# A fused patch-matching and FFN kernel: one-operation squares, relu on ScalarE, and a new call order

## The reference

```python
x = x + conv_ref(ln_c(x), ...)       # match, argmax, gather, mix, 4 small layers
t = to_tokens(x)
t = t + ffn(ln_t(t))                 # ln_t: mean and variance over the 96 channels
# ffn: h = relu(q_acc(q_acc(q_mul(x) @ q_mul(W1).T) + q_mul(b1)))
#      y = q_acc(q_acc(q_mul(h) @ q_mul(W2).T) + q_mul(b2))
```

## Time and profile before

| | |
|---|---|
| median of 3 runs | 2088.41 us (2086.51 to 2092.78) |
| profiled execution | 2092.94 us, of which the span is 2090.8 us |
| mean granted TensorE clock | 0.981 of full speed |
| VectorE busy | 2003.2 us, 96% of the span |
| TensorE busy | 1957.4 us, 94% |
| ScalarE busy | 1829.2 us, 87% |
| GpSimd busy | 1549.9 us, 74% |
| DMA | mean 92 GB/s |
| chain that ended last | 89% on VectorE |

### The profile page before, as it was taken

One profiled execution on the slowest core, in us unless ns is written; L12 is line 12 of the kernel. 1 busy time (PEld: TensorE's weight loads), 2 busy tenths in 40 slices (PEclk: granted clock), 3 DMA queues, 4 the chain that ended last, 5 costly groups with the idle time before them and its releaser, 6 DMA issues.

```text
span 2090.8 us, 46997 instructions
## 1 busy us (share of the span) xinstructions
PE 1957.4 (94%) x13105; PEld 1434.5 (69%) x13105; DVE 2003.2 (96%) x6781; ACT 1829.2 (87%) x5381; POOL 1549.9 (74%) x1042
## 2 busy tenths in 40 slices
PE   5899999999999999999999999999999999999975
PEld 4677777777777777767777777777777777777653
DVE  7999999999999999999999999999999999999953
ACT  1179999999999999999999999999999999999997
POOL 2577877878778777787887777878778778787753
PEclk9999999999999999999999999999999999999985
DMA  3322232332322323323233232232332322323111
GB/s 89 97 78 88 94 106 87 98 102 87 108 91 95 105 87 102 97 91 110 86 97 103 87 107 92 95 105 87 102 97 93 108 86 98 103 87 111 46 40 51
DMA packets 65475, 193.27 MB, mean 92 GB/s; under 512 B 13689, under 2 KB 15939, under 8 KB 65219
## 3 DMA queue, kind: packets, MB, share of 16 engines
q1 hardware_dynamic: 52866, 170.80, 25.2%
q0 software_dynamic: 10240, 18.89, 3.0%
q10 hardware_dynamic: 2112, 0.60, 0.1%
HBM read 133.23 MB, written 57.02 MB: 91 GB/s over the span
## 4 chain that ended last, share of the span: by engine, by line
DVE 89%; issue 6%; PE 3%; ACT 1%; POOL 0%; DMA 0%; POOLq 0%; ACTq 0%; DVEq 0%
DVE best_y L1026 28%; DVE h L1043 13%; DVE stats L1035 9%; DVE t_pm L1051 6%; DVE simraw L1077 6%; DVE top_v L1065 4%; DVE w_index L1072 4%; DVE zb L992 3%; DVE xn L984 1%; DVE mix_in L971 1%; DVE m_dif L929 1%; DVE r_u L1010 1%; DVE ra L1018 1%; DVE one_j L903 1%; DVE r_t L1015 1%
## 5 line engine op out<-in xcount | busy, mean ns | idle before, releaser
L1026 DVE TENSOR_REDUCE best_y<-y_ps 128x2 f32<-128x1024 f32 (+1 forms) x640 | 692.7, 1103 | 4.0 <-PE y_ps L651 3.9
L466 ACT CAST y<-bank 128x384 f16<-128x384 f32 x1152 | 550.5, 478 | 140.8 <-PE bank L674 129.8
L649 PE MATMUL y_ps<-proto_hi,xh 96*128 96x512 f32 x1152 | 553.8, 481 | 22.2 <-DVE best_y L1026 10.4
L359 POOL TENSOR_TENSOR tq<-t_dev,ra 128x864 fp8e5<-128x864 f32 x128 | 209.5, 1637 | 401.3 <-DVE ra L1018 401.3
L650 PE MATMUL y_ps<-proto_lo,xh 96*128 96x512 f32 x1152 | 458.4, 398 | 0.0
L651 PE MATMUL y_ps<-proto_hi,xl 96*128 96x512 f32 x1152 | 457.3, 397 | 0.0
L475 ACT ACTIVATE h<-h 128x1152 fp8e5<-128x1152 f16 x384 | 448.3, 1168 | 0.0
L674 PE MATMUL bank<-tqt,f_w 96*128 96x384 f16 x1152 | 390.4, 339 | 26.5 <-ACT y L466 24.6
L403 POOL TENSOR_TENSOR xl<-xc,xh 96x1152 fp32r<-96x1152 f32 x128 | 339.7, 2654 | 26.4 <-ACT xh L536 15.2
L1043 DVE TENSOR_SCALAR h<-y,f_b 128x1152 f16<-128x1152 f16 x384 | 306.1, 797 | 21.0 <-ACT y L466 20.9
L505 ACT ACTIVATE sq_junk<-t_dev 128x96 f32<-128x96 f32 x1152 | 318.8, 289 | 0.9 <-POOL t_dev L371 0.9
(11 more groups left out here) (131 smaller groups left out, 3997.3 us busy)
## 6 DMA issues: line engine op xcount, KB each, us to landing
xc<-x_cm SPq DMA_DIRECT2D x128, 432.0 KB, 4.0
xp<-x_pm SPq DMA_DIRECT2D x128, 432.0 KB, 4.8
out<-o_pm SPq DMA_DIRECT2D x128, 432.0 KB, 2.5
xsel<-x_pm,x_index POOLq DMA_INDIRECT x128, 2.5
wsel<-proto_rows,w_index POOLq DMA_INDIRECT x128, 4.9
proto_rows<-proto SPq DMA_DIRECT2D x1, 384.0 KB, 2.6
proto<-w_mask SPq DMA_DIRECT2D x1, 192.0 KB, 3.4
f_f<-w_1t ACTq DMA_DIRECT2D x1, 144.0 KB
```

Of the source, the lines that this page charges most:

```text
L466: act.copy(y16[:, q, r, 0:TOK], bank[0][:, 0:TOK]).then_inc(s_y16, 1)
L649: pe.matmul(y, hi, proto_hi[:], start=True, stop=False)
L1026: dve.tensor_reduce(best_y[t % 2][:, j0:j1], y_ps[n % 2][:, 0:j1 - j0, :], AX_X, ALU.max).then_inc(s_yd, 1)
```

## The change

Three edits. The nine squares of a tile on ScalarE, each with a sum read from an accumulator, become one square of all 864 values into t_sq, and VectorE sums them with one reduction (`t_squares`). For q = 0 and 1, bias and relu move from VectorE (`ffn_bias`) to ScalarE (`hidden16`); q = 2 stays on VectorE. And the calls in `slot(s)` of four engines stand in another order; SyncE's order is the same.

```diff
+            def hidden16(s, stage, q):
+                if run.live(s, stage):
+                    t = s - stage
+                    run.wait(s_y16, NC * t + 3 * (q + 1))
+                    run.wait(s_h8, NH * (t - 1) + q + 1)
+                    run.apart()
+                    act.activation(h16[:, q, :, 0:P].rearrange("p (r j) l -> p r j l", r=3),
+                                   y16[:, q, :, 0:TOK].rearrange("p r (j l) -> p r j l", l=P), ACT.Relu,
+                                   bias=f1_b[:, q:q + 1]).then_inc(s_h16[q], 1)
...
-            def squares(s, js):
+            def squares(s):
...
-                        ins = act.activation(sq_junk[:, j * C:(j + 1) * C], t_dev[t % 2][:, j * C:(j + 1) * C],
-                                             ACT.Square, accum_out=va[(s + 1) % 2][:, J + j:J + j + 1])
...
+                    run.wait(s_dev, t + 1)
+                    run.wait(s_sqd, t)
+                    run.apart()
+                    act.activation(t_sq[:], t_dev[t % 2][:], ACT.Square).then_inc(s_sq, 1)
...
+            def t_squares(s):
+                if run.live(s, NORM):
+                    run.wait(s_sq, s - NORM + 1)
+                    ins = dve.tensor_reduce(va[s % 2][:, J:2 * J], t_sq[:].rearrange("p (j c) -> p j c", c=C), AX_X, ALU.add)
+                    ins.then_inc(s_sqd, 1)
...
             def slot(s):
                 lock(s)
                 t_norm(s)
                 product(s)
+                low_h(s)
                 t_center(s)
+                low_x(s)
                 gather_x(s)
+                gather_w(s)
                 output(s)
-                low_x(s)
-                low_h(s)
-                gather_w(s)
```

More of the change, by code:

```diff
@@ L216, in build @@
         s_y16 = sem("y16_ready")
-        s_h16 = sem("h16_ready")
+        s_h16 = [sem(f"h16_ready{q}") for q in range(NH)]
         s_h8 = sem("h8_ready")
@@ L471, in hidden8 @@
                     t = s - stage
-                    run.wait(s_h16, NH * t + q + 1)
+                    run.wait(s_h16[q], t + 1)
                     run.wait(s_f2, 2 * (t - 1))
@@ L566, in slot @@
                 ffn1_out(s, 0)
-                vcs_out(s)
[L568 to L572, removed]
+                high(s)
+                hidden8(s, FFN2, 1)
+                ffn1_out(s, 1)
+                hidden8(s, FFN2, 2)
+                ffn1_out(s, 2)
+                vcs_out(s)
+                hidden16(s, FFN, 0)
+                ffn1_out(s, 3)
+                weighted(s)
+                layer1_out(s)
                 xnt_out(s)
[L574 to L577, removed]
                 turned(s, 0)
                 ffn1_out(s, 4)
+                hidden8(s, FFN, 0)
+                ffn1_out(s, 5)
                 turned(s, 1)
+                mix_out(s)
+                squares(s)
+                ffn1_out(s, 6)
                 hidden1_out(s)
[L582 to L586, removed]
+                hidden16(s, FFN, 1)
+                ffn1_out(s, 7)
                 ffn2_out(s, 0)
-                ffn1_out(s, 7)
+                ffn1_out(s, 8)
                 ffn2_out(s, 1)
-                squares(s, range(4, 7))
-                ffn1_out(s, 8)
-                squares(s, range(7, 9))
             run.slots(slot)
@@ L759, in slot @@
             def slot(s):
-                hidden2(s)
[L761 to L766, removed]
+                match(s, 0)
+                ffn1(s, 0)
+                match(s, 1)
+                conv(s, 0)
+                ffn1(s, 1)
+                match(s, 2)
+                match(s, 3)
+                ffn1(s, 2)
+                hidden2(s)
                 conv(s, 1)
-                match(s, 2)
                 turn_x(s)
-                match(s, 3)
+                layer1(s)
                 ffn1(s, 3)
-                layer1(s)
-                turn_mix(s)
+                match(s, 4)
                 turn(s, 0)
                 ffn1(s, 4)
+                match(s, 5)
                 turn(s, 1)
+                pick(s)
+                ffn1(s, 5)
+                turn_mix(s)
+                match(s, 6)
+                ffn1(s, 6)
+                match(s, 7)
                 hidden1(s)
-                match(s, 4)
-                match(s, 5)
-                ffn1(s, 5)
+                match(s, 8)
                 ffn2(s, 0)
-                pick(s)
-                ffn1(s, 6)
+                ffn1(s, 7)
                 ffn2(s, 1)
-                match(s, 6)
-                ffn1(s, 7)
-                match(s, 7)
                 ffn1(s, 8)
-                match(s, 8)
             run.slots(slot)
@@ L954, in variances @@
                     if run.live(s, NORM):
-                        run.wait(s_sq, s - NORM + 1)
+                        run.wait(s_sqd, s - NORM + 1)
                         run.apart()
@@ L1080, in slot @@
             def slot(s):
+                x_dif(s)
                 low_part(s)
[L1082 to L1083 removed]
                 cos(s)
                 x_sq(s)
[L1086 to L1099 removed]
+                x_sum(s)
+                mix_sims(s)
+                x_norm(s)
+                best_j(s)
+                t_squares(s)
+                ffn_bias(s, FFN2, 2)
+                mix_row(s)
+                variances(s)
+                one_hot(s)
+                root(s, 0)
+                pick_mean(s)
+                root(s, 1)
+                pick_root(s)
+                root(s, 2)
+                ffn2_bias(s)
+                normed_x(s)
                 root(s, 3)
+                remainder(s)
                 root(s, 4)
                 root(s, 5)
[L1103 removed]
+                index(s)
                 root(s, 6)
                 residual(s, 0)
+                y_max(s, 0)
                 residual(s, 1)
                 t_mean(s)
[L1108 to L1109 removed]
                 y_max(s, 1)
[L1111 removed]
                 x_stats(s, [0, 1, 2])
                 x_stats(s, [3, 4])
[L1114 removed]
                 x_stats(s, [5])
                 y_max(s, 2)
+                x_stats(s, [6, 7, 8])
                 best_v(s)
[L1118 to L1119 removed]
+                sims(s)
+                y_max(s, 3)
                 v_index(s)
[L1121 removed]
                 y_max(s, 4)
```

16 lines of the change are left out of this document (5 added, 11 removed).

## The result

| | before | after |
|---|---|---|
| median | 2090.2 us | 2374.1 us (four runs, 2366.1 to 2381.4) |
| ratio | | 1.136, 95% interval 1.131 to 1.140 |
| profiled execution, span | 2092.9, 2090.8 | 2366.1, 2364.3 |
| mean granted TensorE clock | 0.981 | 0.944 |

An execution over 1.5% slower than the fastest of its kernel counts in no median or ratio here; there were two, 7891.55 us of the kernel with the gathers outside and 4793.33 us of the kernel before.

The account below looks back on a forecast made before the run. VectorE's list was taken as the bound, 15.44 us a slot. The xp loop would set 15.08: 116 x 0.36 = 41.8, less 4 for the tail, saves 38 us, giving a median of 2051 us (range 2031 to 2084).

Parts of the forecast that it names:

- GpSimd, "the same eight operations": GpSimd's list keeps its operations and its 12.37 us from tq to the end of the last; output now comes last.
- TensorE, "I take no cost from it": TensorE runs the same instructions in another order; its 14.9 us a slot were given no cost.
- VectorE's list, 14.97: VectorE's work a slot falls from 15.44 to 14.97 us: two bias-and-relu operations leave, one reduction comes.
- ScalarE: Nine squares leave, one square and two relus come: net +0.70 us a slot, busy time 14.22 to 14.92.
- Rival (d): Slower: ScalarE's handshake with TensorE over bank 0 keeps its 0.98 us of waits; 15.90 a slot, median 2145; chance 0.09 with late xp.
- SyncE and xp: On the SyncE queue out, xc and xp are issued in one run; xp lands 5.13 us after issue (4.8 to 6.0).
- The wait it forecast: VectorE waits for xp at the first statistics operation, 0.11 us a slot.
- My two loops: Slot periods through xp's landing: one over two slots, 15.08 us; one through the w index and gather, 14.78 us.
- Ramp and tail: First slots unchanged; added ScalarE work after slot 127 costs at most 10.3 us, taken as 4.

Follow-up runs that it names:

- the kernel with the gathers outside: Changed kernel with GpSimd's gather_x first and gather_w last, VectorE's one-input operations ahead of its small two-input ones; the last and fastest kernel built: 2076.6 us, ratio 0.994.
- the old orders: Kernel before with the square, the sum and the two relus, but each engine's other calls ordered as before: 2168.1 us, ratio 1.038.
- both moves: Changed kernel with GpSimd's output ahead of gather_w, and t_squares and ffn_bias moved to the head of VectorE's slot: 2117.9 us, ratio 1.013.

## Why the prediction was wrong

It said 2051 us (2031 to 2084), and none of its rivals was this case. By its own steps:

1. **GpSimd, "the same eight operations".** This step failed. I summed its list apart from VectorE's and priced the new place of `output` only through the store behind it. The place decides which operation of VectorE runs beside it. The list by itself was nearly right: 12.75 us from tq to the end of `output` (1007.58 to 1020.33), forecast 12.37. In the kernel before, GpSimd waits for `lock` for 3.00 us ahead of tq, and VectorE's small two-input operations stand in that pause and beside the gather ahead of it: the cover was an idle time, and I read it as slack. In the changed kernel `output` lies where they are. The missing term is 2.28 us a slot, 17.16 in place of 14.88, and a hold comes with GpSimd's order alone: in the kernel before it makes `low_part` 1.86 us longer and the slot 17.23. The Trainium skill, SBUF — State Buffer, section "Who interferes with whom", states the rule: VectorE's second pair of SBUF ports is GpSimd's, and a lock on it makes one wait for the other, for VectorE instructions with two SBUF inputs but not for reductions. By that page the hold would have been a rival; the traces agree (held at 0.59 to 2.53 us with two inputs, 0.16 with one; sums 1.03 as ever).
2. **TensorE, "I take no cost from it".** Wrong by 62 us: in the changed kernel its clock falls to the lower level in 36 slots and makes them longer. The experiment with more matmuls takes 55 of these 62 us away.
3. **VectorE's list, 14.97.** Right in its size: 14.92 in the ramp of the changed kernel, 14.88 worked out from its full slots; 15.16 in the last kernel, which has VectorE as its bound. There dependent small operations leave gaps (the last root starts at 1014.52, 0.22 after the one ahead of it) that a sum over a differently mixed list doesn't hold.
4. **ScalarE.** Right: the relu took 1.245 us busy (forecast 1.28), the square 0.94 (0.89), the sum on VectorE 1.03 (1.03). Rival (d), the handshake over bank 0, doesn't decide the changed kernel but does show with the old orders (ratio 1.038).
5. **SyncE and xp.** Right in size: out, xc and xp are issued 0.4 apart, and xp lands after 4.9 (forecast 5.13). The wait it forecast isn't there, because a slot of 17.16 hides it; it came with the hold away, 0.37 us a slot with one-input `x_norm`, 9.6 us with both moves. My two loops named the transfer and the gather's issue, but not the landing of wsel, 2.7 or 5.2 us by its place, whose loop comes to 15.2 to 15.5.
6. **Ramp and tail.** I took 0 and 4; they are 5.3 and 8.2, and 7.0 and 6.7 in the best kernel, half of what its full slots win.

Sum: 5.3 + 198 + 62 + 8.2 = 273.5. Left open: why `x_norm` is held from 1000.65 on, 0.64 us before `output`'s record begins, and why it is then VectorE that waits and not GpSimd. The gather alone doesn't hold it: in the ramp, with the gather but without `output`, `x_norm` takes 0.17 (63.56 and 155.11). Nor was it tried why the clock fell in 36 slots and not in all, or what the square and the relu are worth each by itself.

## What to carry to other kernels

VectorE's and GpSimd's lists can't be summed apart when both work on SBUF: write beside each GpSimd operation which VectorE operations will run next to it, and put reductions and one-input operations there. An idle time of GpSimd may be the cover under which VectorE's two-input operations run, so look at what runs in a pause before filling it. A hold isn't in the list of waits; it shows as an operation whose mean is far above its minimum, here a mean of 2177 ns where the shortest took 157, for nine values a partition.

## What the runs showed of the hardware

- In eight kernels a small VectorE operation with two SBUF inputs (0.15 to 0.31 us by itself) lasted up to 2.54 us beside GpSimd's arithmetic and ended within 0.2 us of the end of GpSimd's operation. Halving GpSimd's `output` (1.85 to 1.02) shortened the median `x_norm` by as much, 0.83. GpSimd's whole `output` kept its 1.82 to 1.87 us in every kernel.
- VectorE operations with one SBUF input were not held beside GpSimd's: a reduction of 128 x 864 (1.04), a relu (0.80), an addition of a bank and an SBUF tile (0.65).
- In the long slot shown, TensorE was busy for 0.32 to 0.06 us of the half microseconds from 384.5 to 386, and the granted clock stood at its lower level from 387.5 to 394. Of 115 slots, 36 had a lower clock, and all 36 were long. Matmuls that only repeat work made the kernel 61 us faster.
- The same gather landed after 2.7 us when issued by itself and 5.2 beside the store and two loads.
